# Weights loaded in place, two transposed input tiles and a new dealing-out of the work at the phase boundaries, in a fused attention and MLP kernel

## The chip, the cores and the metric

One core of a Trainium2 chip runs the whole program. The time is the device time of one execution in microseconds, median of the runs shown. TensorE is called PE here, VectorE DVE, ScalarE ACT, GpSimd POOL; SP is the engine that issues the transfers.

## What is computed

x is 16 batches of 128 tokens by 512 numbers, enc the same shape. Two layers follow each other, all in float32:

```
ln  = layernorm(x);   q, k, v = split(ln @ w_qkv + b_qkv)
x   = x + attention(q, k, v, mask_a) @ w_ao + b_ao            # stage A
q   = layernorm(x) @ w_q + b_q;  k, v = split(enc @ w_kv + b_kv)
x   = x + attention(q, k, v, mask_b) @ w_co + b_co            # stage B
x   = x + gelu(layernorm(x) @ w1 + b1) @ w2 + b2              # MLP
a   = layernorm(enc)
x   = x + tanh(gate) * (attention(x @ Wq.T, a @ Wk.T, a @ Wv.T, key mask) @ Wo.T)   # stage D
```

Each attention has 16 heads of 32; in stages A and B the scores are multiplied by the mask and get -10000 * (1 - mask) before the softmax; the gelu is the one with tanh.

## The kernel before, in words

**Products.** Each float32 product is made of three PE passes over split operands: hi by hi, hi by lo, lo by hi. So each weight exists twice on chip, in `weights_hi` and `weights_lo`. The weights are 20 units of 512 x 512, each of four chunks of 128 x 512, which pass in turn through 8 slots. A chunk is loaded by SP (`load_chunk`, L403) into one of four stage buffers, `weights_raw`; ACT rounds it into `weights_hi` (`split`, L980), and POOL (L1735) or, at the start and at the end of the MLP, DVE (L1310) subtracts and writes `weights_lo`. The stage buffer is then free for another chunk. ACT also waits for the slot to be free (`slot_free`).

**Fills.** Inputs come in fills of 256 tokens. For a layer-norm fill, SP loads two tiles, DVE takes the statistics (L1319), POOL the inverse deviation, DVE normalises (`normalise`, L1327, two instructions), SP stores the result to memory (L370) and loads it back with the roles of rows and columns exchanged in blocks (`load_transposed`, L393, four transfers) into the one tile `inputs_transposed`. DVE turns the 32 x 32 blocks in that tile (`turn_inputs`, L1334), ACT applies scale and bias (`fill_scale`, L1078), DVE rounds to the high part (`fill_hi`, L1358) and POOL subtracts the low part (`fill_lo`, L1754). Raw fills, of enc in B and of the stream in D, skip the layer norm. The next transposed load waits until the fill before it has left the tile.

**Steps.** A, B and D have 16 steps each, one batch per step; the batch in the step is called g, 0 to 47 over the three stages. In a step PE makes, in this order: probabilities by v for g-2 (L672), scores of g (L621), one unit of a projection for a later fill (L599, L605), a small product that lays out the row sums of g-1 (L655), two of four transposes of the probabilities of g-1 (L639), a second unit, the other transposes, a third unit, and the output projection of g-2 (L696). DVE and ACT bring out what PE made: `mask_scores` (L1384), POOL `add_mask_bias` (L1764), DVE `row_max` (L1397), ACT `exps` (L1043, 16 instructions), DVE `inverse_sums` (L1405), and from the projections ACT `half_out` for queries and keys (L1009, L1013) and DVE `v_out` for values (L1435). The order on each engine is written out by hand and semaphores alone join them, so an instruction that waits holds up all that stands behind it on its engine.

**Joints.** The MLP works on 64 pairs p: w1 (L752) makes a piece of the hidden layer, ACT `hidden_out` (L1121, L1127) and `tanh` (L1108), DVE the rest of the gelu (L1459 to L1476), w2 (L776) its share of the output. Its first pairs run within the last steps of B (`last_steps_of_b`), and the first projections of D run within its last pairs. There the regular order breaks: in B the steps b = 12 to 15 have fewer projection units left, twelve weight chunks of units 11 to 14 are loaded and split late (table `LATE`), and at the end of the MLP the splits of units 16 to 18 are dealt out by `LAST_SPLITS`.

The lines that set the order of a fill and a chunk in the step of SP are these:

```
if st.weight:
    load_chunk(st.weight)
...
if st.ahead:
    load_transposed(st.ahead)
```

## Time and profile before

| | us |
|---|---|
| Median of three runs | 1167.53 (1167.33 to 1167.87) |
| The profiled execution | 1163.93 |
| Its span | 1162.6 |
| PE busy | 1118.7 (96%) |
| DVE busy | 830.8 (71%) |
| ACT busy | 721.5 (62%) |
| POOL busy | 460.9 (40%) |

The granted clock of PE was 0.997 of full over the profiled execution. Stage A fills about 33 to 281 us of the span, B reaches to about 547, overlapping with the MLP that ends about 903, and D starts within the MLP's last pairs and ends with the span. The table says how much of the span each engine worked, not what it waited for; the waits are read from the rows below.

### The profile page before, as it was taken

What the parts mean: (1) busy time and instruction counts of PE and PEld (TensorE: products, weight loads), DVE (VectorE), ACT (ScalarE), POOL (GpSimd) and SP (SyncE); (2) the same over time, 40 slices, a digit from 0 to 9 for tenths busy, and PEclk for the clock granted to TensorE, in tenths of its full rate; (3) what the DMA queues carried; (4) which work ended last, traced back from release to release, by engine and by line L of the source; (5) the groups of instructions that cost most, each with busy time, mean ns of one, the idle gap of its engine ahead of it and who ended that gap; (6) DMA issues with size and microseconds to landing.
All of it is one profiled execution on the core that took longest, in us unless ns stands there. A gap on an engine that the chain in (4) does not pass through costs nothing.

```text
span 1162.6 us, 26097 instructions
## 1 busy us (share of the span) xinstructions
PE 1118.7 (96%) x9701; PEld 998.1 (86%) x9701; DVE 830.8 (71%) x1351; ACT 721.5 (62%) x2450; POOL 460.9 (40%) x337
## 2 busy tenths in 40 slices
PE   7899999999999999889999999999999989999998
PEld 6788888988888889777799999999998888888886
DVE  6677777677777887797766566655668487777677
ACT  4577776767787777677444434434445286777766
POOL 3675565556667776567412112111111421222100
PEclk9999999999999999899999999999999999999999
DMA  6334443345544445645230230330425445555422
GB/s 205 113 107 121 127 119 93 111 133 147 144 141 135 140 143 148 159 118 160 90 92 19 73 91 1 91 91 1 127 64 160 102 83 130 126 129 123 97 79 83
DMA packets 226238, 128.36 MB, mean 110 GB/s; under 512 B 169680, under 2 KB 177088, under 8 KB 226112
## 3 DMA queue, kind: packets, MB, share of 16 engines
q1 hardware_dynamic: 226112, 126.69, 39.3%
q8 instruction: 78, 1.28, 0.4%
q14 instruction: 48, 0.39, 0.1%
HBM read 93.75 MB, written 32.89 MB: 109 GB/s over the span
## 4 chain that ended last, share of the span: by engine, by line
PE 62%; DVE 12%; ACT 11%; issue 4%; DMA 3%; POOL 3%; SPq 2%; DVEq 0%; ACTq 0%; POOLq 0%
PE psum L605 13%; PE psum L776 13%; PE psum L752 13%; PE psum L696 7%; ACT prob L1043 6%; PE psum L599 5%; PE psum L639 4%; PE psum L621 3%; DVE ln_tile L1327 2%; ACT inputs_transposed L1078 2%; PE psum L672 2%; DVE prob L1384 2%; POOL prob L1764 1%; SPq L393 1%; DMA weights_raw<-weights_in 1%
## 5 line engine op out<-in xcount | busy, mean ns | idle before, releaser
L1043 ACT ACTIVATE prob<-prob,negmax 128x128 f32<-128x128 f32 x768 | 296.8, 393 | 25.6 <-DVE negmax L1397 25.5
L1754 POOL TENSOR_TENSOR inputs_lo<-inputs_transposed,inputs_hi 128x512 fp32r<-128x512 f32 x92 | 124.6, 1374 | 367.0 <-DVE inputs_hi L1358 295.4
L605 PE MATMUL psum<-inputs_hi,weights_hi 128*128 128x256 f32 x768 | 224.6, 292 | 4.6 <-POOL inputs_lo L1754 1.9
L605 PE MATMUL psum<-inputs_lo,weights_hi 128*128 128x256 f32 x768 | 217.0, 283 | 0.0
L605 PE MATMUL psum<-inputs_hi,weights_lo 128*128 128x256 f32 x768 | 216.9, 282 | 0.0
L1764 POOL TENSOR_TENSOR prob<-prob,mask_bias 128x1024 f32<-128x1024 f32 x64 | 155.4, 2450 | 135.6 <-DVE prob L1384 133.5
L605 PEld LDWEIGHTS psum<-inputs_hi,weights_hi 128*128 128x128 f32 x768 | 146.6, 191 | 9.5 <-issue 2.8
L1043 ACT ACTIVATION_READ_ACCUMULATOR prob<-prob,negmax 128x1 f32 x768 | 148.0, 193 | 0.0
L605 PEld LDWEIGHTS psum<-inputs_lo,weights_hi 128*128 128x128 f32 x768 | 146.9, 191 | 0.2
L605 PEld LDWEIGHTS psum<-inputs_hi,weights_lo 128*128 128x128 f32 x768 | 146.8, 191 | 0.0
L752 PE MATMUL psum<-inputs_hi,weights_hi 128*128 128x256 f32 x512 | 145.0, 283 | 1.0 <-POOL inputs_lo L1754 1.0
L752 PE MATMUL psum<-inputs_lo,weights_hi 128*128 128x256 f32 x512 | 144.9, 283 | 0.0
L752 PE MATMUL psum<-inputs_hi,weights_lo 128*128 128x256 f32 x512 | 144.9, 283 | 0.0
L1397 DVE TENSOR_REDUCE negmax<-prob 128x8 f32<-128x1024 f32 x96 | 113.4, 1199 | 17.2 <-POOL prob L1764 17.1
L1121 ACT ACTIVATE qT<-psum,columns 128x256 f32<-128x256 f32 x128 | 53.4, 469 | 112.7 <-PE psum L752 112.7
L1476 DVE SCALAR_TENSOR_TENSOR kT<-kT,qT 128x512 f32<-128x512 f32 x64 | 53.0, 829 | 92.1 <-ACT kT L1127 91.9
L776 PE MATMUL psum<-weights_hi,context_hi 128*128 128x512 f32 x256 | 101.4, 396 | 5.7 <-DVE context_lo L1471 5.5
L752 PEld LDWEIGHTS psum<-inputs_hi,weights_hi 128*128 128x128 f32 x512 | 98.0, 191 | 3.6 <-issue 1.2
L639 PE MATMUL psum<-identity,prob 128*128 128x128 f32 x752 | 98.2, 273 | 2.8 <-ACT prob L1032 2.4
L776 PE MATMUL psum<-weights_lo,context_hi 128*128 128x512 f32 x256 | 100.4, 392 | 0.0
L752 PEld LDWEIGHTS psum<-inputs_lo,weights_hi 128*128 128x128 f32 x512 | 98.0, 191 | 2.3
L776 PE MATMUL psum<-weights_hi,context_lo 128*128 128x512 f32 x256 | 99.7, 389 | 0.0
(112 smaller groups left out, 2526.6 us busy)
## 6 DMA issues: line engine op xcount, KB each, us to landing
weights_raw<-weights_in SPq DMA_DIRECT2D x72, 256.0 KB, 4.0
normalised<-ln_tile SPq DMA_DIRECT2D x30, 512.0 KB, 2.8
inputs_transposed<-normalised SPq DMA_DIRECT2D x120, 128.0 KB, 3.4
stream<-residual SPq DMA_DIRECT2D x48, 256.0 KB, 2.9
residual<-stream SPq DMA_DIRECT2D x48, 256.0 KB, 3.8
context<-row_sums_spread SPq DMA_DIRECT2D x188, 64.0 KB, 2.0
ln_tile<-stream SPq DMA_DIRECT2D x32, 256.0 KB, 3.8
ln_tile<-x_in SPq DMA_DIRECT2D x16, 256.0 KB, 3.4
```

The lines of the kernel that those rows point to most:

```text
L599: mm = pe.matmul(ps[:, bank, :], a[:, buf, c, tok], w[:, slot, c, :], start=c == 0 and i == 0, stop=c == KC - 1 and i == 2)
L605: mm = pe.matmul(ps[:, bank, GT * part:GT * part + GT], w[:, slot, c, o], a[:, buf, c, :], start=c == 0 and i == 0, stop=c == KC - 1 and i ...
L639: mm = pe.transpose(ps[:, bank, T * j:T * j + T], prob[:, g % 2, s:s + T], ident[:, :])
L696: mm = pe.matmul(ps[:, U_BANK + 1, :], a[:, 0, cs], w[:, slot, c, :], start=c == 0 and i == 0, stop=c == KC - 1 and i == 2)
L752: mm = pe.matmul(ps[:, bank, GT * e:GT * e + GT], w[:, slot, c, o], a[:, gp, c, :], start=n == 0, stop=n == 3 * KC - 1)
L776: mm = pe.matmul(ps[:, acc, :], a[:, gb, tok], w[:, slot, 2 * (j % 2) + e, :], start=j == 0 and n == 0, stop=j == NPAIR - 1 and n == 5)
L1043: ins = act.activation(P[:, T * s:T * s + T], P[:, T * s:T * s + T], ACT.Exp, bias=negmax[:, par, s:s + 1], accum_out=total[:, par, s:s + 1])
L1121: ins = act.activation(hx(p)[:, GT * e:GT * e + GT], ps[:, bank, GT * e:GT * e + GT], ACT.Identity, bias=cols[:, col:col + 1])
L1397: dve.tensor_reduce(negmax[:, par, 8 * h:8 * h + 8], heads(prob[:, par, 1024 * h:1024 * h + 1024]), AX.X, ALU.max, negate=True).then_inc(s ...
L1476: dve.scalar_tensor_tensor(hw(p), hw(p), 1.0 / GELU_A, hx(p), ALU.add, ALU.mult).then_inc(s_in, 1)
L1754: pool.tensor_tensor(xlo[:, fill.buf, :, tokens(t)], y, xhi[:, fill.buf, :, tokens(t)].bitcast(f32), ALU.subtract).then_inc(s_rlo if fill. ...
L1764: pool.tensor_tensor(half, half, mb.unsqueeze(1).to_broadcast([128, 8, T]), ALU.add).then_inc(s_biased, 1)
```

## The change

**Weights.** The stage buffers are gone. A chunk is loaded straight into the place where its low part will stand: `weights_whole` is a plain float32 view of the memory of `weights_lo`. ACT reads it there for `weights_hi`, and the subtraction overwrites it in place. So SP, not ACT, now waits for the slot to be free, and the chunk of the following step is loaded a step ahead. `LATE` is gone: B loads two chunks in steps 5 and 11, units 13 and 12 at the end of step 13, unit 14 after step 15; the units 16 to 19 have new places and splits, more of them on DVE.

**Fills.** `inputs_transposed` has two tiles, used in turn; a transposed load waits for the fill two before it.

**Order.** In B, steps 12 and 13 take three units instead of two, and 14 and 15 none: two pairs of w1 stand in their place. The DVE's `normalise` moves behind the row maxima, `turn_inputs` behind the first of them. ACT brings out the second unit before `fill_scale`. In D the first two steps of ACT are written out anew. PE makes the same products.

```diff
@@ attention_steps, steps of B
+        elif phase == B and b < 14:
+            units = [(phase, 7, n) for n in ((0, 1, 2), (4, 5, 3))[odd]]
...
-        elif phase == B:
-            units = [None, (phase, 7, (2, 3)[odd]), None]
...
+        elif phase == B and b < 14:
+            chunks = [b + (b > 5) + (b > 11)] + ([b + 1 + (b > 5)] if b in (5, 11) else [])
...
-LAST_SPLITS = {2: (16, 0), 3: (16, 2), 4: (17, 0), 5: (17, 2), 6: (18, 0), 7: (18, 2)}
+LAST_SPLITS = {3: (16, 0), 4: (16, 2), 5: (17, 0), 6: (17, 2), 7: (18, 0)}
@@ build, tiles
         whi = sb("weights_hi", [128, SLOTS, KC, H], f32r)
+        with nc.sbuf_tensor("weights_whole", [128, SLOTS, KC, H], f32) as raw:
+            pass
         wlo = sb("weights_lo", [128, SLOTS, KC, H], f32r)
-        raw = sb("weights_raw", [128, STG, H])
...
-        xt = sb("inputs_transposed", [128, KC, GT])
+        xt = sb("inputs_transposed", [128, 2, KC, GT])
...
-            return g in (0, 28, 32, 44)
+            return g in (0, 32, 44)
@@ SP
             def load_transposed(fill):
-                was = PREVIOUS[fill]
+                was = FILLS[FILLS.index(fill) - 2]
...
+            def slot_free(unit):
+                if unit in (8, 9, 10, 11):
+                    sp.wait_ge(s_half, half_count(A, 7, 5))
...
+                if unit in (16, 18):
+                    sp.wait_ge(s_h, 60 if unit == 18 else 58)
+                if unit in (17, 19):
+                    sp.wait_ge(s_w2, 58 if unit == 17 else 60)
             def load_chunk(chunk):
...
-                sp.dma_start(raw[:, buf, :], weights[chunk[0], chunk[1], :, :]).then_inc(s_raw[buf], 16)
+                sp.dma_start(raw[:, slot_of(unit), c, :], weights[unit, c, :, :]).then_inc(s_raw[k], 16)
...
-                if st.weight:
-                    load_chunk(st.weight)
+                for chunk in following.weights if following else []:
+                    load_chunk(chunk)
...
-                if st.phase == B and st.b >= 13:
-                    for chunk in LATE[st.b + 1][:3]:
-                        load_chunk(chunk)
+                if st.phase == B and st.b == 13:
+                    for unit in (13, 12):
+                        for c in range(KC):
+                            load_chunk((unit, c))
...
-                    unit = {(0, 6): 15, (6, 7): 16, (7, 2): 17, (7, 5): 18}.get((g, jp))
+                    unit = {(0, 6): 15, (7, 2): 16, (7, 3): 17, (7, 5): 18}.get((g, jp))
...
             load_transposed(raw_fill(D, 0, 0))
+            load_transposed(ln_fill(3, 1, 1))
...
-            load_transposed(ln_fill(3, 1, 1))
             load_transposed(STEPS[D][0].fill)
@@ PE, last_steps_of_b
-                    if b == 14:
-                        row_sums_out(28)
                     w1_bank_free(2 * b - 28)
                     w1(2 * b - 28)
                     row_sums(g - 1)
                     transpose_prob(g - 1, 0)
                     transpose_prob(g - 1, 1)
                     row_sums_out(g - 1)
-                    project(*unit, U_BANK + 1)
+                    w1(2 * b - 27)
                     transpose_prob(g - 1, 2)
                     transpose_prob(g - 1, 3)
-                    w1_bank_free(2 * b - 27)
-                    w1(2 * b - 27)
-                    half_out(*unit)
+                    pe.wait_ge(s_hx, 2 * b - 26)
                     project_out(g - 2)
                 times_v(30)
-                w2(0)
+                w1_bank_free(4)
+                w1(4)
                 row_sums(31)
                 transpose_prob(31, 0)
                 transpose_prob(31, 1)
+                w2(0)
@@ ACT, step
+                if st.fill and st.fill not in TURNED:
+                    fill_hi(st.fill)
+                if not st.prev or (st.ends and not late):
+                    half_out(*st.units[1])
+                if st.fill in TURNED:
+                    fill_out(st.fill)
+                if st.prev:
+                    prob_out(g - 1, 2)
+                if not st.ends:
+                    half_out(*st.units[2])
                 exps(g, 0)
...
@@ DVE, step
-                if st.ahead and st.ahead.ln is not None:
+                if ahead_ln and later_ln:
                     normalise(st.ahead)
-                if st.fill in TURNED:
-                    turn_inputs(st.fill)
-                row_max(g, 0)
+                if st.ends or not st.prev:
+                    row_max(g, 0)
+                    if st.fill in TURNED:
+                        turn_inputs(st.fill)
...
                 if st.prev:
                     prob_out(g - 1, 3)
+                if ahead_ln and not later_ln:
+                    normalise(st.ahead)
@@ DVE, end of the MLP
-                if g == NG - 1 and jp in LAST_SPLITS:
+                if g == NG - 1 and jp in (3, 4):
                     unit, c = LAST_SPLITS[jp]
                     split((unit, c))
                     split((unit, c + 1))
             turn_inputs(raw_fill(D, 0, 0))
             gelu_hi(NG * NPAIR - 1)
             gelu_lo(NG * NPAIR - 1)
+            for unit in (17, 18):
+                for c in range(KC):
+                    split((unit, c))
             mlp_out(NG - 1)
```

DVE in an odd step of stage A, where the fill ahead is normalised (`ln_tile` is its tile, `negmax` the row maxima, `v` the values of a projection). Before:

```order
L1384 SCALAR_TENSOR_TENSOR prob<-psum,mask 128x512 x4
L1410 COPY prob<-psum 128x512
L1327 TENSOR_SCALAR ln_tile<-ln_tile,ln_mean_var,ln_rstd 128x512 x2
L1397 TENSOR_REDUCE negmax<-prob 128x8
L1435 TENSOR_TENSOR v<-psum,bias_rows 128x512
L1397 TENSOR_REDUCE negmax<-prob 128x8
L1410 COPY prob<-psum 128x512
L1435 TENSOR_TENSOR v<-psum,bias_rows 128x512
L1447 TENSOR_TENSOR residual<-psum,residual 128x512
```

After:

```order
L1380 SCALAR_TENSOR_TENSOR prob<-psum,mask 128x512 x4
L1406 COPY prob<-psum 128x512
L1393 TENSOR_REDUCE negmax<-prob 128x8
L1431 TENSOR_TENSOR v<-psum,bias_rows 128x512
L1393 TENSOR_REDUCE negmax<-prob 128x8
L1406 COPY prob<-psum 128x512
L1322 TENSOR_SCALAR ln_tile<-ln_tile,ln_mean_var,ln_rstd 128x512 x2
L1431 TENSOR_TENSOR v<-psum,bias_rows 128x512
L1443 TENSOR_TENSOR residual<-psum,residual 128x512
```

The two `normalise` instructions moved behind both row maxima and the first of the two `v_out`.

DVE in step 12 of stage B, before:

```order
L1384 SCALAR_TENSOR_TENSOR prob<-psum,mask 128x512 x4
L1410 COPY prob<-psum 128x512
L1327 TENSOR_SCALAR ln_tile<-ln_tile,ln_mean_var,ln_rstd 128x512 x2
L1334 STREAM_TRANSPOSE inputs_transposed<-inputs_transposed 128x1024
L1397 TENSOR_REDUCE negmax<-prob 128x8 x2
L1410 COPY prob<-psum 128x512
L1358 CAST inputs_hi<-inputs_transposed 128x4x128 x2
```

The same place after:

```order
L1380 SCALAR_TENSOR_TENSOR prob<-psum,mask 128x512 x4
L1406 COPY prob<-psum 128x512
L1393 TENSOR_REDUCE negmax<-prob 128x8
L1329 STREAM_TRANSPOSE inputs_transposed<-inputs_transposed 128x1024
L1393 TENSOR_REDUCE negmax<-prob 128x8
L1406 COPY prob<-psum 128x512
L1322 TENSOR_SCALAR ln_tile<-ln_tile,ln_mean_var,ln_rstd 128x512 x2
L1353 CAST inputs_hi<-inputs_transposed 128x4x128 x2
```

The turn no longer stands behind `normalise`; the fill that is turned here was normalised a step earlier, and the one that is normalised here is the next.

ACT in step 14 of stage B, the first with MLP work in it (`qT` and `kT` hold the hidden layer there), before:

```order
L1064 ACTIVATE context_hi<-context 128x256 x2
L1052 ACTIVATE row_sums_transposed<-psum 16x128
L1032 ACTIVATE prob<-psum 128x512
L980 ACTIVATE weights_hi<-weights_raw 128x512 x3
L1121 ACTIVATE qT<-psum,columns 128x256 x2
L1127 ACTIVATE kT<-qT 128x512
L1043 ACTIVATE prob,total<-prob,negmax 128x128 x4
L1032 ACTIVATE prob<-psum 128x512
L1043 ACTIVATE prob,total<-prob,negmax 128x128 x4
L1121 ACTIVATE qT<-psum,columns 128x256 x2
L1127 ACTIVATE kT<-qT 128x512
L1043 ACTIVATE prob,total<-prob,negmax 128x128 x8
```

The same place after:

```order
L1049 ACTIVATE context_hi<-context 128x256 x2
L1037 ACTIVATE row_sums_transposed<-psum 16x128
L1106 ACTIVATE qT<-psum,columns 128x256 x2
L1112 ACTIVATE kT<-qT 128x512
L1017 ACTIVATE prob<-psum 128x512
L980 ACTIVATE weights_hi<-weights_whole 128x512 x2
L1106 ACTIVATE qT<-psum,columns 128x256 x2
L1112 ACTIVATE kT<-qT 128x512
L1017 ACTIVATE prob<-psum 128x512
L1028 ACTIVATE prob,total<-prob,negmax 128x128 x16
```

Three chunk splits became two, and both `hidden_out` stand ahead of the sixteen exponentials.

## Rows read from the trace of the kernel before

**Rows 1.** Windows: stretch, length; busy PE, PEld, DVE, ACT, POOL; clock; DMA share; GB/s

```profile
40.00:62.00 22.00, 17.62 (x191) 15.24 (x191) 15.47 (x25) 16.21 (x68) 14.90 (x10) 1.00 0.41 116
62.00:470.00 408.00, 404.48 (x3998) 359.91 (x3998) 315.09 (x518) 301.49 (x1170) 260.00 (x172) 1.00 0.46 131
470.00:530.00 60.00, 51.06 (x478) 44.34 (x478) 48.67 (x71) 41.90 (x150) 37.03 (x23) 0.94 0.50 142
530.00:585.00 55.00, 49.88 (x343) 42.59 (x342) 43.57 (x54) 30.49 (x81) 29.22 (x20) 1.00 0.33 105
585.00:885.00 300.00, 300.00 (x1928) 274.00 (x1927) 186.23 (x298) 127.06 (x246) 47.14 (x42) 1.00 0.24 68
885.00:955.00 70.00, 62.56 (x513) 55.96 (x512) 47.58 (x75) 37.75 (x115) 23.66 (x20) 1.00 0.49 118
```

**Rows 2.** Timeline, 471 to 481 us (start, length, instruction, idle before)

```profile
471.77 4.89 POOL L1764 TENSOR_TENSOR prob<-prob,mask_bias 128x1024 f32<-128x1024 f32 x2 [2.46 <-DVE prob L1384]
...
473.40 3.54 DVE L1327 TENSOR_SCALAR ln_tile<-ln_tile,ln_mean_var,ln_rstd 128x512 f32<-128x512 f32 x2
476.87 1.23 DVE L1334 STREAM_TRANSPOSE inputs_transposed<-inputs_transposed 128x1024 f32<-128x1024 f32 x1
...
478.13 2.07 ACT L1078 ACTIVATE inputs_transposed<-inputs_transposed,columns 128x256 f32<-128x256 f32 x4 [3.35 <-DVE inputs_transposed L1334]
...
480.98 0.79 PE L696 MATMUL psum<-weights_hi,context_hi 128*128 128x512 f32 x1 [5.55 <-ACT kT L1013]
```

**Rows 3.** Windows, line L696 alone, the stretch right behind that wait

```profile
481.00:486.50 5.50, 5.46 (x12) 3.77 (x12) 0.50 0.19 30
```

**Rows 4.** Waits of PE, 530 to 585 us (total, times, longest)

```profile
PE psum L776 <- DVE context_lo L1471: 4.0, 4, 1.2
PE psum L696 <- DVE context_lo L1421: 1.0, 1, 1.0
```

**Rows 5.** Part 5 of the page, the exponentials on ACT

```profile
L1043 ACT ACTIVATE prob<-prob,negmax 128x128 f32<-128x128 f32 x768 | 296.8, 393 | 25.6 <-DVE negmax L1397 25.5
```

**Rows 6.** Waits of PE, 85 to 190 us

```profile
PE psum L696 <- DVE v L1435: 3.0, 4, 1.3
```

**Rows 7.** Waits of PE, 885 to 955 us

```profile
PE psum L621 <- ACT qT L1009: 2.6, 2, 2.0
PE psum L776 <- DVE context_lo L1471: 1.5, 2, 1.0
```

**Rows 8.** Timeline, SP and DVE at the end of the MLP

```profile
872.08 18.39 SPq L403 DMA_DIRECT2D weights_raw<-weights_in  x8
...
916.12 1.25 DVE L1334 STREAM_TRANSPOSE inputs_transposed<-inputs_transposed 128x1024 f32<-128x1024 f32 x1 [10.12 <-DMA inputs_transposed<-normalised]
```

**Rows 9.** Timeline of DVE, two instructions with and without POOL beside them

```profile
862.45 0.99 DVE L1327 TENSOR_SCALAR ln_tile<-ln_tile,ln_mean_var,ln_rstd 128x512 f32<-128x512 f32 x2
...
886.63 3.49 DVE L1310 TENSOR_TENSOR weights_lo<-weights_raw,weights_hi 128x512 fp32r<-128x512 f32 x2
```

**Rows 10.** Timeline, two steady steps of stage B, 396 to 425 us

```profile
396.38 3.07 DVE L1327 TENSOR_SCALAR ln_tile<-ln_tile,ln_mean_var,ln_rstd 128x512 f32<-128x512 f32 x2
...
403.12 2.78 SPq L393 DMA_DIRECT2D inputs_transposed<-normalised  x4
...
411.75 1.23 DVE L1334 STREAM_TRANSPOSE inputs_transposed<-inputs_transposed 128x1024 f32<-128x1024 f32 x1
...
413.69 2.07 ACT L1078 ACTIVATE inputs_transposed<-inputs_transposed,columns 128x256 f32<-128x256 f32 x4
...
414.92 1.22 DVE L1397 TENSOR_REDUCE negmax<-prob 128x8 f32<-128x1024 f32 x1 [0.84 <-POOL prob L1764]
...
422.44 0.26 DVE L1405 RECIPROCAL rtotal<-total 128x16 f32<-128x16 f32 x1 [1.67 <-ACT prob L1043]
...
424.20 0.27 PE L655 MATMUL psum<-identity,rtotal 128*16 128x128 f32 x1
```

**Rows 11.** Part 6 of the page: transfers, KB each, us from issue to landing

```profile
inputs_transposed<-normalised SPq DMA_DIRECT2D x120, 128.0 KB, 3.4
```

More of the change, by code:

```diff
@@ L15 @@
 SLOTS = 8
-STG = 4
 EPS = 1e-5
@@ L42 @@
 Fill = namedtuple("Fill", "ln phase q buf n")
-Step = namedtuple("Step", "phase b prev ends units fill weight ahead later")
+Step = namedtuple("Step", "phase b prev ends units fill weights ahead later")
 def ln_fill(ln, q, buf):
@@ L1501, in step @@
                     context(g - 2, 1)
+                if st.ends and not late and phase == D:
+                    make_mask_bias(g)
+                    mask_scores(g, 0)
+                if st.ends and not late:
                     inverse_sums(g - 1)
@@ L1718, in dve_program @@
             gelu_lo(NG * NPAIR - 1)
+            for unit in (17, 18):
+                for c in range(KC):
+                    split((unit, c))
             mlp_out(NG - 1)
```

292 lines of the change are left out of this document (136 added, 156 removed).

## The prediction

> **What bounds the kernel now.** First the windows. PE is busy 300.00 us of the 300 in the middle of the MLP and 404.48 of 408 from 62 to 470 us [rows 1]. Since the change leaves PE the same products, nothing is to be won where PE never stops; the time can only come out of its gaps. They lie together: 4.38 us between 40 and 62, 3.52 from 62 to 470, 8.94 in 470 to 530, 5.12 in 530 to 585 and 7.44 in 885 to 955 [rows 1], 29.4 in all. The other engines are at most 71% busy, so a gap is an order in which something stands too late. The waits and the timeline then say which order. What is in those gaps is the most that the change can win, beside a clock that falls behind one of them.
>
> **The change part by part, end of B and entry of the MLP.** The largest gap ends at 480.98 after 5.55 us: the first product of an output projection waits for the kT copy of ACT [rows 2]. The timeline shows why. DVE's two normalise instructions start at 473.40 and take 3.54 us beside POOL's mask additions (471.77, 4.89), the turn of another fill stands behind them at 476.87, and ACT, which has idled 3.35 us for that turn, does fill_scale from 478.13 for 2.07 us and only then the copy [rows 2]. The change undoes this twice: the turn no longer stands behind a normalise in that step, and the copy stands ahead of fill_scale. Without fill_scale ahead of it alone the copy could come at least 5 us earlier, so I take the gap as gone. Behind the gap the 12 products of that line took 5.46 us at a granted clock of 0.50, that is 1.2 of the two levels 1.2 and 2.4 GHz [rows 3]. Halving that gives 2.73 back; the bounds are 0 (another gap drops the clock as well) and 2.73, and I take it whole, since no other gap in these stretches is as long.
>
> The rest of the idle time of 470 to 530 is 3.4 us in small waits, and 530 to 585 has four waits of w2 for the gelu, 4.0 us, and one of 1.0 [rows 4]. Steps 14 and 15 now have two w1 pairs in place of pair and unit, both hidden copies ahead of the exponentials, and two splits instead of three. So the gelu is earlier and w2 should wait little. In exchange the exponentials, which are 296.8 us over 48 steps, so 6.2 a step [rows 5], start later: behind two hidden copies, a projection's worth of ACT work that was spread through them. ACT's chain of a step is then about as long as PE's work in it, and I leave 1.9 us for row sums and products with v of the last two steps that wait for it, and 3 us for small waits: about 5 stay of 14.1. The sum for this part is -(14.1 - 5) - 2.7 = -11.8; call it **-12**. The end least favourable, only the 5.55 gap and no clock, is -5.5.
>
> **Stage A.** Between 85 and 190 us PE waits four times, 3.0 us, for the `v` copy of DVE [rows 6]; in each of these steps the copy stands behind a normalise of up to 3.58 us beside the additions. The change puts the first of the two copies ahead of the normalise and I take these 3.0 as gone, with 0.3 of smaller ones: **-3.3**. The bounds are 0, if the second copy, still behind the normalise, is as late, and -3.5. In the first steps, where 4.38 us are lost [rows 1], g = 1 gets the turn and the copies ahead; what is left is the wait for the first row sums, which is a chain of exponentials that the change leaves. I take **-1.5**, between 0 and -4.4.
>
> **End of the MLP and entry of D.** SP now waits for the fill two before, and the last layer-norm fill of D is loaded right behind the first raw one instead of behind residuals and chunks. Before, DVE idled 10.12 us for it until 916.12 [rows 8], and ACT's qT copy behind it held PE for 2.6 us in two waits [rows 7]. That wait goes, and with it most of 5.9 us of gaps without w2 in that stretch; I leave 1, so about -5. Against it stand the weights. Before, eight chunk loads took 18.39 us to issue, from 872.08, since each waited for a stage buffer [rows 8]; now they are issued when the slot is free, unit 16 one pair later than before, and ACT's split in pair 3 of the last group stands behind their landing. What is queued behind that split is the gelu chain that w2 waits for, 1.5 us in two waits already [rows 7]. I add 1.4 us. The eight splits that DVE gets in one run before `mlp_out(7)` cost between 4 (two of another form in 0.99) and 14 us (two in 3.49 beside POOL) [rows 9]; they lie beside PE's first projections of D and, as long as those last, at nothing. Net **-3.6**, between -6 and +2.
>
> **Steady steps of B.** Here the change costs. The normalise starts at 396.38 now and ends 399.45, the transposed loads are issued from 403.12 to 405.90, and their turn stands at 411.75 [rows 10]; a load lands 3.4 us after its issue [rows 11]. Moved behind both row maxima and a copy the normalise starts about 401.0, and takes 0.99 to 3.58 us [rows 2, 9], so it ends 2.6 to 5.1 us later than now. Against this stand some 3.1 us of slack at the turn (411.75 less the landing of the fourth load, about 405.2 + 3.4), and 1.9 more since the turn itself moves behind a row maximum: the second waits 0.84 for POOL until 414.92, the first can start one addition (2.45) earlier, at about 412.5, and the turn ends at 414.9 instead of 413.0 [rows 2, 10]. So the loads should just be in time. fill_scale then starts at 414.9 and not at 413.69, 1.2 us later; the row sums are ready at 422.7 and PE takes them at 424.20, which leaves 1.5 [rows 10]. So the shift is hidden with 0.3 us to spare. That cover is thin, and I book **+0.5** for all such steps, between 0 and +9 (13 layer-norm fills by 0.7). Stage A has the same order, but there fill_scale already stands behind copies, so I book nothing.
>
> The normalise takes 0.99 us alone at 862.45 and 3.54 beside the additions [rows 2, 9]. The Trainium skill, SBUF — State Buffer, "Who interferes with whom", says that DVE and GpSimd share a port pair that one holds for a whole instruction while the other fully blocks. By that rule the moved normalise, now beside POOL's `fill_lo` and residual bias, would wait for whole instructions of POOL, which speaks for the late end of the range above and gives the rival of lateness below; the rows agree in size, but none here shows the pair at the new place.
>
> **In place loading.** It removes no work of ACT, DVE or POOL. The chunks of A and B are loaded a step ahead; where ACT waited for landings between copies it now doesn't, and this lies beside PE's work: nothing, both ways.
>
> **Sum**: -12 - 3.3 - 1.5 - 3.6 + 0.5 = -19.9. The profiled execution took 1163.93 us, 3.6 under the median 1167.53; its own time would become 1144.0. Against the median that is **1148 us**, rounded up as all the terms lean on whole gaps.
>
> **Rivals.** (a) *Lateness in the LN fills*: the moved normalise delays store, loads and turn beyond the slack in the steps with a layer-norm fill, at 0.7 us in 13 of them: +9, so about 1157. For it: 0.3 us to spare and DVE beside POOL. Against it: the load slack grows with the turn. (b) *The boundaries pay half*: ACT's exponentials bound the last steps of B and unit 16 comes late, so 6 to 7 of the 15.6 us of the two boundaries stay: 1154 or 1155. For it: ACT's chain there is as long as PE's. (c) *Slower*: SP's queue. Normalise late means that store, four loads, row sums' store and spread behind them on SP are all late, so that DVE's context waits as well as its turn, in all layer-norm fills of A, B and D, some 20. It decides from 1.05 us per fill beyond the slack, where it eats the 20 us; at 1.5 us it is +30 - 20: 1177. Against it: the spread has other time, and the largest shift found is 5.1 against 5.0. (d) *It doesn't do what it says*: the gaps only move, since PE waits for what was second latest each time: about 1167. Against it: the largest gap has two causes and both are removed.
>
> **How the numbers follow.** Forecast case 0.62 (1142 to 1152), (a) 0.17, (b) 0.14, (c) 0.04, (d) 0.03. The low end is 1142, where A's first steps and the entry of the MLP give all they have; the high end 1158 takes in (a) and (b). About 0.2% or 2.3 us is what a measurement of this kernel can tell from no change. Faster than 1165.2 by that: 0.93; within: 0.03; slower: 0.04.
>
> **What would show it.** The windows 470 to 530 and 530 to 585 with PE at some 95% and a clock near 1.00; no wait of L696 for kT above 1 us; in stage A no waits for `v`; DVE's idle time at D's second turn gone. Wrong: in each second step of B a gap at the row sums, or waits of the turn for its transfer, say (a); a wait of ACT's split for weights in the last group with w2 idle says (b); spread transfers waited for by DVE in every pair say (c).

## The result: 1137.85 us, and the profile after

The changed kernel took 1137.85 us (median of 4, 1137.55 to 1138.20) against 1167.43 of the kernel before in the same comparison (4 runs, 1166.68 to 1167.87): a ratio of 0.9747, 95% interval 0.973 to 0.9764. The forecast was 1148, range 1142 to 1158. The direction was right, the gain half as large again as forecast, and the range missed.

The profiled execution took 1137.63 us with a span of 1136.3. PE is busy 1112.6 us of it (98%), DVE 826.8, ACT 719.5, POOL 459.7. The windows of the changed kernel around the places that [rows 1] show (columns as there):

```profile
40.00:62.00 22.00, 19.90 (x210) 17.32 (x209) 17.39 (x30) 19.30 (x81) 15.06 (x11) 1.00 0.46 118
467.00:520.00 53.00, 52.02 (x526) 45.94 (x525) 47.31 (x72) 45.41 (x174) 36.65 (x24) 1.00 0.54 156
520.00:570.00 50.00, 46.16 (x293) 39.63 (x292) 37.96 (x49) 24.45 (x53) 28.82 (x20) 1.00 0.26 87
865.00:925.00 60.00, 57.48 (x477) 51.59 (x476) 46.22 (x69) 38.46 (x114) 24.34 (x20) 1.00 0.46 108
```

PE idles 2.10 us in the first steps (4.38 before), 0.98 and 3.84 around the end of B (8.94 and 5.12), and 2.52 at the entry of D (7.44); the clock is 1.00 in all of them, where [rows 1] had 0.94. The waits of PE from 520 to 570 us, where [rows 4] had 4.0 and 1.0:

```profile
PE psum L782 <- DVE context_lo L1467: 1.7, 2, 1.6
PE psum L678 <- ACT prob L1017: 0.8, 1, 0.8
PE psum L758 <- POOL weights_lo L1746: 0.8, 1, 0.8
PE psum L661 <- DVE rtotal L1401: 0.5, 1, 0.5
```

To see where time went, the starts of the same PE product in the two traces serve better than windows. These are the rows of the changed kernel (timeline of PE; start and length first), the first scores of batches 5, 16, 28, 35, 44 and 47 and the first w2 product of pairs 8 and 57:

```profile
105.29 0.39 PE L627 MATMUL psum<-kT,qT 32*128 32x128 f32 x4
...
274.44 0.39 PE L627 MATMUL psum<-kT,qT 32*128 32x128 f32 x4
...
459.36 0.39 PE L627 MATMUL psum<-kT,qT 32*128 32x128 f32 x4
...
573.02 0.40 PE L782 MATMUL psum<-weights_hi,context_hi 128*128 128x512 f32 x1
...
848.39 0.40 PE L782 MATMUL psum<-weights_hi,context_hi 128*128 128x512 f32 x1
...
938.17 0.39 PE L627 MATMUL psum<-kT,qT 32*128 32x128 f32 x4
...
1076.86 0.39 PE L627 MATMUL psum<-kT,qT 32*128 32x128 f32 x4
...
1113.35 0.39 PE L627 MATMUL psum<-kT,qT 32*128 32x128 f32 x4
```

| up to | before at | after at | stretch won | forecast |
|---|---|---|---|---|
| scores of batch 5 | 108.79 | 105.29 | 3.50 | 1.5 |
| batch 16 | 280.85 | 274.44 | 2.91 | 3.3 |
| batch 28 | 466.46 | 459.36 | 0.69 | -0.5 |
| w2 of pair 8 | 593.04 | 573.02 | 12.92 | 12 |
| w2 of pair 57 | 868.42 | 848.39 | 0.01 | 0 |
| batch 35 | 963.16 | 938.17 | 4.96 | 3.6 |
| batch 44 | 1101.85 | 1076.86 | 0.00 | 0 |
| batch 47 | 1139.64 | 1113.35 | 1.30 | 0 |
| end of the span | 1162.6 | 1136.3 | 0.0 | 0 |

Batch here is g, counted over the three stages. The stretches add up to 26.3 us, where the sum had 19.9. The other 3.3 of the 29.6 lie between the profiled execution of before (1163.93) and its timed runs.

The place of the largest gap, [rows 2], reads like this now (timeline, DVE, then ACT, then PE, in step 12 of B):

```profile
468.75 1.23 DVE L1329 STREAM_TRANSPOSE inputs_transposed<-inputs_transposed 128x1024 f32<-128x1024 f32 x1
...
471.71 1.00 DVE L1322 TENSOR_SCALAR ln_tile<-ln_tile,ln_mean_var,ln_rstd 128x512 f32<-128x512 f32 x2
...
467.47 0.84 ACT L998 ACTIVATE kT<-psum,columns 128x256 f32<-128x256 f32 x2 [1.76 <-PE psum L611]
470.02 2.08 ACT L1063 ACTIVATE inputs_transposed<-inputs_transposed,columns 128x256 f32<-128x256 f32 x4 [1.72 <-DVE inputs_transposed L1329]
...
470.89 0.39 PE L702 MATMUL psum<-weights_hi,context_hi 128*128 128x512 f32 x1
```

ACT's copy runs at 467.47, ahead of fill_scale, the turn stands behind one row maximum only, and the normalise, now behind both and with POOL idle beside it, takes 1.00 us instead of 3.54. The third unit gives PE work from 468.06 on, and it goes into its output projection at 470.89 without a wait.

### The profile page after: what moved, and what is told of

The parts are those of the page before. It is cut to its first block, busy times and chain, and to the rows that moved or that the text cites. A ratio compares the mean times of both kernels' runs of the same rounds, so it can differ in the third digit from the quotient of the medians.

```text
span 1136.3 us, 26121 instructions
## 1 busy us (share of the span) xinstructions
PE 1112.6 (98%) x9701; PEld 996.5 (88%) x9701; DVE 826.8 (73%) x1351; ACT 719.5 (63%) x2450; POOL 459.7 (40%) x337
## 4 chain that ended last, share of the span: by engine, by line
PE 78%; DVE 7%; ACT 7%; DMA 3%; issue 2%; POOL 2%; SPq 1%; DVEq 0%; ACTq 0%
PE psum L611 20%; PE psum L758 13%; PE psum L782 13%; PE psum L702 9%; PE psum L605 9%; PE psum L645 6%; PE psum L627 4%; ACT prob L1028 4%; PE psum L678 3%; POOL prob L1775 1%; ACT inputs_transposed L1063 1%; DMA weights_whole<-weights_in 1%; DMA normalised<-ln_tile 1%; DVE context_lo L1467 1%; DVE prob L1380 1%
## 5 line engine op out<-in xcount | busy, mean ns | idle before, releaser
L1775 POOL TENSOR_TENSOR prob<-prob,mask_bias 128x1024 f32<-128x1024 f32 x64 | 153.0, 2413 | 119.5 <-DVE prob L1380 117.5
```

The source lines that it names most:

```text
L1775: pool.tensor_tensor(half, half, mb.unsqueeze(1).to_broadcast([128, 8, T]), ALU.add).then_inc(s_biased, 1)
```

## The experiments

Ratios are to the kernel before, run on the same chip, with their 95% intervals; for edits of the changed kernel the distance to its own 1137.85 (1138.03 when it ran again, below) says more. The kernel before had medians of 1164.4 to 1165.6 in these later comparisons. Labels that begin with b_ are the kernel before with an edit, those with a_ the changed kernel with one.

**The largest gap by itself, in the kernel before.** First both swaps in g = 28:

```diff
@@ DVE, step
+                if g == 28:
+                    turn_inputs(st.fill)
                 if st.ahead and st.ahead.ln is not None:
                     normalise(st.ahead)
-                if st.fill in TURNED:
+                if st.fill in TURNED and g != 28:
                     turn_inputs(st.fill)
@@ ACT, step
+                if g == 28:
+                    half_out(*st.units[1])
                 if st.fill and not regular:
                     fill_out(st.fill)
-                if not st.prev or not (st.units[2] or late):
+                if not st.prev or (not (st.units[2] or late) and g != 28):
                     half_out(*st.units[1])
```

> The kernel before with two changes in step 12 of stage B alone (g = 28): DVE turns ahead of normalise, ACT copies the second unit ahead of fill_scale. Theory 1: the whole 5.55 us gap goes and the clock with it, and the 3.5 us by which the timed runs of before lie over its profiled execution are also a clock lost behind this gap; then the median falls by 5.5 + 2.7 + 3.5 = 11.7 us, to about 1156, and the span of the profiled execution by 8.3. Theory 2: those 3.5 us belong to timed runs as such (or to something else in the program); then the median falls by 8.3, to about 1159. Theory 3: the gap only moves to the row sums or to the gelu; then under 3 us are won.

Measured: 1161.17 us (1159.19 to 1165.82), ratio 0.997 (0.9956 to 0.9985). Theory 3 came nearest: 3.3 us, and the gap moved. Its timeline (DVE, ACT, ACT, PE; the profiled execution is the slowest of its eleven) shows what it moved to:

```profile
475.85 3.67 DVE L1329 TENSOR_SCALAR ln_tile<-ln_tile,ln_mean_var,ln_rstd 128x512 f32<-128x512 f32 x2
...
480.69 0.40 ACT L1043 ACTIVATE prob<-prob,negmax 128x128 f32<-128x128 f32 x1 [2.00 <-DVE negmax L1399]
...
482.24 0.57 ACT L1032 ACTIVATE prob<-psum 128x512 f32<-128x512 f32 x1
...
482.87 1.51 PE L672 MATMUL psum<-prob,v 128*32 128x128 f32 x24 [3.05 <-ACT prob L1032]
```

The exponentials wait 2.00 us for row maxima that stand behind a normalise of 3.67; the copy of the third block of probabilities (L1032), which this step put behind the first quarter of the exponentials, comes at 482.24; PE waits 3.05 us for it. So the gap had a third cause behind the two that I had found. Then the ACT part of that diff alone (b_act28) and the DVE part alone (b_dve28):

> The kernel before with ACT's copy ahead of fill_scale in g = 28 and nothing else. If the copy's place alone made the gap, this is worth all that both are worth (8.3 to 11.7 us). If the late turn still holds fill_scale, the exponentials and the row sums of g = 28, 2 to 4 us come back as a wait one step later and 5 to 8 are won.

> The kernel before with DVE's turn ahead of normalise in g = 28 and nothing else. fill_scale then ends at about 476.7 instead of 480.2 and the copy at 477.5, so a gap of some 2 us stays; 3.5 us are won if the clock still falls behind it, 6 to 9.5 if it doesn't. The other theory (normalise beside POOL just blocks elsewhere, and the next fill is late): nothing won.

Measured: ACT's swap 1163.51 us, ratio 0.9994 (0.9982 to 1.0006), nothing that can be told; DVE's 1161.51, ratio 0.9967 (0.9956 to 0.9979), 2.9 us. With ACT's swap alone the same product by v waits 4.05 us. Theories with 5 us and more fall for both.

**The changed kernel with one part undone.**

First DVE's order:

```diff
@@ DVE, step
-                if ahead_ln and later_ln:
+                if ahead_ln:
                     normalise(st.ahead)
                 if st.ends or not st.prev:
-                    row_max(g, 0)
                     if st.fill in TURNED:
                         turn_inputs(st.fill)
+                    row_max(g, 0)
...
-                if ahead_ln and not later_ln:
-                    normalise(st.ahead)
```

> The changed kernel with DVE's normalise back ahead of the row maxima and the turn back ahead of the first row maximum. By my account this gives back the 2.9 us of stage A (waits for v) and, in g = 28 and 29, what the turn behind normalise costs: with ACT's copy ahead of fill_scale only 0 to 3 us there. So 1141 to 1144. Rival: the DVE order is what removes the big gap, then 1146 or more. B's steady steps: no difference by either.

Measured: 1143.96 us, ratio 0.982 (0.9801 to 0.9839): 6.1 us back. By the starts of the scores 2.8 of them lie in stage A, where the wait for `v` returns (first row below, 85 to 190 us, against [rows 6]), 0.8 at the end of B, and 2.5 in D's second step, where the second row's wait is new:

```profile
PE psum L702 <- DVE v L1431: 2.2, 4, 0.6
...
PE psum L605 <- ACT v L1007: 2.4, 1, 2.4
```

Then ACT's, with the rule of before for `regular` steps:

```diff
@@ ACT, step
-                if st.fill and st.fill not in TURNED:
-                    fill_hi(st.fill)
-                if not st.prev or (st.ends and not late):
-                    half_out(*st.units[1])
-                if st.fill in TURNED:
-                    fill_out(st.fill)
...
+                if st.fill and not regular:
+                    fill_out(st.fill)
+                if not st.prev or not (st.units[2] or late):
+                    half_out(*st.units[1])
+                if late:
+                    prob_out(g - 1, 2)
+                if regular:
+                    half_out(*st.units[1])
+                if st.fill and regular:
+                    fill_out(st.fill)
```

> The changed kernel with the order of ACT's step as before (second unit behind fill_scale where the third is missing, second and third unit among the exponentials in the first steps). All steps 12 and 13 of B have three units now, so the old rule takes its regular branch there and the big gap does not come back: 1138 to 1139. What comes back is the first steps: 0.5 to 1.5 us. Rival: ACT's order carries the boundary, then 1143 or more.

Measured: 1139.59 us, ratio 0.9779 (0.9763 to 0.9795): 1.7 us back, 1.2 of them in D's step 12, where the copy stands behind fill_scale again (not in the first steps, as expected), and none at the end of B.

One tile instead of two:

```diff
-TILE_OF = {_fill: _n % 2 for _n, _fill in enumerate(FILLS[2:])}
+TILE_OF = {_fill: 0 for _fill in FILLS[2:]}
...
-                was = FILLS[FILLS.index(fill) - 2]
+                was = FILLS[FILLS.index(fill) - 1]
```

> The changed kernel with one transposed tile again: each load waits for the fill just before it. In B's steady steps the loads landed 0.17 us before the turn could use them with two tiles, so if the second tile is what lets them be in time, each layer-norm fill of B loses, and D's second fill is late again as before: 3 to 5 us lost at D and 0 to 5 in B, so 1141 to 1148. Rival: the store of the normalised tile, not the free tile, sets the load (it waits 3.5 us for the store's landing), so only the entry of D loses, or nothing: 1138 to 1141.

Measured: 1140.66 us, ratio 0.9788 (0.9772 to 0.9804): 2.8 us back, all but a few tenths at D's entry. In B's steps one is 0.3 us longer and the others are as they were: from 285 to 460 us SP waits 12.2 us for the stores of normalised tiles to land and 0.7 for the tile to be free, so the store sets the load there, not the tile.

The place of one load:

```diff
             load_transposed(raw_fill(D, 0, 0))
-            load_transposed(ln_fill(3, 1, 1))
...
             load_tiles(ln_fill(3, 2, 1))
+            load_transposed(ln_fill(3, 1, 1))
             load_transposed(STEPS[D][0].fill)
```

> The changed kernel with the transposed load of the last layer-norm fill of D back behind the residual and chunk loads. If its early place is what won the 5 us at D's entry, 3 to 5 us come back: 1141 to 1143. If the second tile alone did it, nothing.

Measured: 1148.24 us, ratio 0.9853 (0.9838 to 0.9869): 10.4 us back, more than any theory said. The wait of PE between 855 and 930 us, and the clock in it:

```profile
PE psum L611 <- ACT v L1007: 9.4, 1, 9.4
...
904.00:907.00 3.00, 1.83 (x8) 1.83 (x9) 2.30 (x7) 1.60 (x4) 1.82 (x2) 0.50 0.04 6
```

PE waits 9.42 us for a `v`, since in the changed order ACT's fill_scale of that fill stands ahead of that copy and waits for the load, and PE goes on at a clock of 1.2 GHz. The early load is not a bonus there; the new ACT order needs it.

**The units of B's last steps.**

ACT's and DVE's order in steps 14 and 15 is the old one too, as far as these units need it: the hidden copies stand among the exponentials again.

```diff
         elif phase == B and b < 14:
-            units = [(phase, 7, n) for n in ((0, 1, 2), (4, 5, 3))[odd]]
+            units = [(phase, 7, (0, 4)[odd]), (phase, 7, (1, 5)[odd]), None]
+        elif phase == B:
+            units = [None, (phase, 7, (2, 3)[odd]), None]
@@ PE, last_steps_of_b
-                    w1(2 * b - 27)
+                    project(B, 7, b - 12, U_BANK + 1)
                     transpose_prob(g - 1, 2)
                     transpose_prob(g - 1, 3)
+                    w1_bank_free(2 * b - 27)
+                    w1(2 * b - 27)
```

> The changed kernel with the projection units of B's last four steps dealt as before: two in steps 12 and 13, one in 14 and 15, with the first w1 pairs, the hidden copies and the copy of that unit in their old places; weights in place, two tiles, DVE and ACT orders of the regular steps as in the change. Theory 1, from the first four of these runs: a step of B with two units gives PE 12.5 us of work against some 13 of ACT with its exponentials, so PE waits in step 12 for the copies of the probabilities, whatever stands in front of them; the third unit is what fills the gap. Then 6 to 12 us come back: 1144 to 1150, with a wait before the products with v at g = 28 and more at w2. Theory 2: the orders of the regular steps and the weights in place carry it: under 3 us come back.

Measured: 1142.78 us, ratio 0.981 (0.9796 to 0.9823): 4.9 us back, 4.4 of them by the trace between batch 28 and the first w2. Waits of PE from 465 to 570 us:

```profile
PE psum L684 <- ACT prob L1025: 3.2, 3, 1.6
PE psum L788 <- DVE context_lo L1475: 1.7, 2, 1.5
PE psum L617 <- POOL inputs_lo L1774: 1.0, 1, 1.0
```

The products with v wait 3.2 us for copied probabilities. Between the two theories: the units, with the order of steps 14 and 15 that goes with them, carry 4.4 of the 12.9 us, not 6 to 12.

**The load a step ahead.** In the changed kernel without it (a_own_step), and in the kernel before with it (b_ahead), both in SP's step:

```diff
@@ a_own_step
-                for chunk in following.weights if following else []:
+                for chunk in st.weights if g else []:
                     load_chunk(chunk)
@@ b_ahead
-                if st.weight:
-                    load_chunk(st.weight)
+                following = (STEPS[A] + STEPS[B])[g + 1] if g < 31 else None
+                if g == 0:
+                    load_chunk(st.weight)
+                if following and following.weight:
+                    load_chunk(following.weight)
```

> The changed kernel with each chunk of A and B loaded in its own step instead of the one before. If the landing of a chunk, which ACT waited for between copies, cost time before, 1 to 5 us come back and the runs spread again over several microseconds as those of before do (1160.8 to 1168.3). If it was hidden, as the prediction has it: 1138, spread under 1.5.

> The kernel before with its four stage buffers, each chunk of A and B loaded in the step before its own; nothing else. Theory 1: the ACT of before hides its chunk waits in the old order (its waits for chunks are 27.6 us in all and PE hardly stops there), so the load ahead alone wins 0 to 2 us, and is only what allows the new order. Theory 2: the load ahead is itself the gain: 5 us or more, with the spread of the runs gone.

Measured: a_own_step 1165.52 us (1162.71 to 1168.12), ratio 1.0004 (0.9991 to 1.0016). The changed kernel loses 27.5 us by it, far more than either theory said. b_ahead 1163.97 us, ratio 0.9985 (0.9976 to 0.9994): 1 us. The waits of ACT for chunks, in the changed kernel and in a_own_step:

```profile
ACT weights_hi L980 <- DMA weights_whole<-weights_in: 11.1, 6, 5.4
```

```profile
ACT weights_hi L980 <- DMA weights_whole<-weights_in: 78.9, 20, 6.7
```

78.9 us against 11.1 (27.6 in the kernel before). In the new order `split` stands ahead of the copies of the projection, so a chunk that lands late holds up what PE waits for: from batch 4 to 28 most steps are 0.5 to 2.3 us longer, one 3.9, 27.0 in sum. This is a loss that the kernel before doesn't have (its batch 28 starts at 466.46 us, that of a_own_step at 487.10); the gain behind batch 28 stays, and that the two cancel to a ratio of 1.00 is chance. Theory 1 holds for b_ahead: early loading wins next to nothing in the old order. It is the condition of the new one.

Two more go on from b_ahead: b_ahead28 adds the two swaps of the first diff, and b_orders the change's regular order of ACT and DVE for all steps:

```diff
@@ ACT, step
-                if not st.prev or not (st.units[2] or late):
+                if not st.prev or (st.ends and not late):
                     half_out(*st.units[1])
...
@@ DVE, step
+                if ahead_ln and later_ln:
+                    normalise(st.ahead)
+                row_max(g, 0)
                 if st.fill in TURNED:
                     turn_inputs(st.fill)
-                row_max(g, 0)
...
+                if ahead_ln and not later_ln:
+                    normalise(st.ahead)
```

> The same load ahead, and the two swaps in g = 28 (turn ahead of normalise, copy ahead of fill_scale). The swaps alone won 3.3 us. If the chunk's landing was the next thing late there, together they win clearly more than the two apart: 6 to 9. If the missing third unit is, 3 to 5.

> The kernel before with the load ahead and the regular step orders of ACT and DVE from the change; stage buffers, one tile, the old units in B's last steps and the old MLP end stay. Stage A should win its 2.9 us, g = 28 the big gap less what two units leave (about 5 of the 12.9 us of that boundary by the run with the old units), so 8 to 11 us: 1154 to 1157. If it wins under 5, the places of loads and splits around the boundary (table LATE) carry the rest.

Measured: b_ahead28 1159.83 us, ratio 0.9958 (0.9945 to 0.9972): 5.1 us, at the end of the 3 to 5 that the missing third unit was to leave. b_orders 1162.98 us, ratio 0.9983 (0.9974 to 0.9991): 1.9 us only. Its trace has the gains that were expected: 2.7 us ahead up to batch 16, and 6.2 won from batch 28 to w2 of pair 8, of which 2.7 are the clock that doesn't fall there. But it loses 2.9 again in the first steps of B (a wait of 2.23 for a copy of probabilities on DVE) and 6.0 from batch 32 to 44. D's steps lack the change's earlier mask and its second tile there; which of them it is was not tested. So the order of steps pays only with more of the change around it.

**D's entry in the kernel before.**

```diff
             load_transposed(raw_fill(D, 0, 0))
+            load_transposed(ln_fill(3, 1, 1))
...
             load_tiles(ln_fill(3, 2, 1))
-            load_transposed(ln_fill(3, 1, 1))
```

> The kernel before with one thing moved: the transposed load of the last layer-norm fill of D right behind the first raw one, still with one tile. The 2 us wait before the first scores of D goes and with it the clock that falls behind it in some executions: 3 to 6 us won. Rival: with one tile the load waits for the raw fill to leave it, and SP with it, so that residual and chunk loads behind it are late: nothing won, or slower.

Measured: 1161.40 us (1159.58 to 1162.52), ratio 0.9967 (0.9956 to 0.9979): 3.9 us. The largest wait of the first scores fell from 2.0 [rows 7] to 0.9.

**The gaps that are left.**

a_split16 puts ACT's four splits of unit 16 in pair 4 behind fill_scale, and DVE's in pair 5. a_plus2 puts both in pair 4, ACT's ahead of fill_scale, and moves two transposes:

```diff
@@ a_plus2: ACT, loop over the pairs (DVE the same, in pair 4)
+                if g == NG - 1 and jp == 4:
+                    for c in range(KC):
+                        split((16, c))
                 if jp == (5 if g == 0 else 4):
                     fill_scale(FILLS_OF_MLP[g] or mlp_fill(1))
...
-                if g == NG - 1 and jp in LAST_SPLITS:
+                if g == NG - 1 and jp > 4:
@@ a_plus2: PE, last_steps_of_b
-                project_out(30)
                 transpose_prob(31, 2)
                 transpose_prob(31, 3)
+                project_out(30)
```

a_plus has besides, on ACT and POOL, unit 14 split before 13, and unit 15 in pair 5 ahead of fill_scale and of fill_lo.

> The changed kernel with the four splits of unit 16 at one place, a pair later on ACT (in pair 4 of the last group) and in pair 5 on DVE. ACT no longer waits 5.39 us for the landing of the first chunk in pair 3. If that wait is what costs 0.56 of w2 there, it goes; four splits in a row take ACT 2.3 us and may cost as much a pair later: 1136.5 to 1139.

Measured: 1138.54 us, ratio 0.9771 (0.9757 to 0.9786), no better: one wait of w2 of 2.24 us for two of 0.56 and 1.02, with a granted clock of 0.67 in the 4 us around its end (872 to 876 us).

> The changed kernel with five moves at gaps that its trace still shows: unit 14 split before 13 (w1 waits 0.78 us for POOL), unit 15 split a pair earlier and ahead of fill_scale and fill_lo (w2 waits 1.54), the last two transposes of batch 31 ahead of the output projection of 30 (0.83), and the four splits of unit 16 together in pair 4 ahead of fill_scale, where ACT idles for the turn (0.56 and 1.02). If each gap goes and none comes new: 4.4 us, about 1133.5. If POOL's splits beside DVE's gelu just slow it a pair earlier: 2 us or less.

Measured: 1137.46 us, ratio 0.9763 (0.975 to 0.9775). By the trace the transposes won 0.9 and the splits of unit 16 2.0. From batch 28 to w2 of pair 8 the kernel is all the same 2.6 us longer than a_plus2, the next run, which has these two moves and not the splits of 13 to 15. Part of that is DVE beside POOL a pair earlier, as the second theory said: the waits of w2 there are 4.0 us in sum and not 1.8. The rest is a granted clock that falls to 0.73 around the end of the longest of them (556 to 560 us), less a wait of w1 of 0.8 that is gone.

> The changed kernel with only the two moves that won in the run before: the last two transposes of batch 31 ahead of the output projection of 30, and the four splits of unit 16 together in pair 4 ahead of fill_scale on ACT. Units 13 to 15 are split where the change has them. In the traces those two were worth 0.9 and 2.1 us, so 1134.6 to 1135.3, a clock of 1.00 and a spread under 1.5 us.

> The changed kernel as it is, again, on the chip of the run beside it: 1137 to 1138.5, with the kernel before at 1161 to 1168 on the same chip. If the chips of the first runs were unlike, the ratio of 0.9747 moves by the 2 to 3 us by which the first four runs of before lie over the later ones.

Measured: a_plus2 1135.16 us (1134.82 to 1135.78), ratio 0.9742 (0.9729 to 0.9756); a_same 1138.03 (1137.62 to 1138.49), ratio 0.9766 (0.9753 to 0.9779), before 1165.56 (1162.98 to 1166.53). a_plus2 is 2.9 us faster than the change and the fastest version here. The change itself is worth 27.5 us in this comparison; the first runs of before lay at the upper end of what it does.

## Why the prediction was wrong

**What bounds the kernel.** Right: PE's work is the same, and the gain came at the places listed. PE's idle time fell by 20.2 us (from 43.9 to 23.7), and its busy time by 6.1, of which 2.7 are the clock behind the largest gap. What failed is the sum, in two steps. First, its terms were too small: -19.9, where the same stretches gave -26.3. The first steps gave 2.0 us more than booked, D's entry 1.4, the steady steps of B 1.2, the end of B 0.9, and the end of D 1.3 for which there was no term; stage A gave 0.4 less. Second, "Against the median that is 1148 us" added the 3.6 between one profiled execution and the median as if it were a constant; measured, these 3.3 us came back on top. The terms weigh more: without the constant the forecast is 1144.0, still 6.2 too high.

**One execution and the median.** In later runs before took 1160.8 to 1168.3 us, with medians 2 to 3 us under the first one, and the change 1137.6 to 1138.5. So the distance is no constant; it lies within a spread that the changed kernel doesn't have. In the profiled execution of before only one gap was followed by the lower clock [rows 3]. In b_dve28, which differs from it in one place of DVE's order, the clock isn't down there but behind a w2 wait and at D's entry (windows, columns as in [rows 1]):

```profile
555.00:558.00 3.00, 3.00 (x9) 2.28 (x9) 2.27 (x4) 0.63 (x1) 0.00 (x0) 0.53 0.84 288
919.00:925.00 6.00, 5.20 (x46) 5.01 (x39) 5.80 (x11) 1.14 (x4) 5.92 (x7) 0.72 0.57 90
```

Of the seven profiles of the kernel before and its edits that load D's last fill as before, five show the lower clock there; before and b_both28 don't. So each execution loses the clock behind another few of its gaps, while the changed kernel's two profiled runs had 1.00 throughout. In the 85 later runs of before the time goes with the mean clock: a median of 1166.4 us at 0.991 to 0.993 (13 runs), 1165.2 at 0.994 (37) and 1163.9 above (35). It isn't all of it. The runs at 0.994 alone lie up to 5 us apart (1163.1 to 1168.3), and a_own_step spreads from 1162.7 to 1168.1 at clocks of 0.996 to 1.000, its slowest run at 0.999. What the rest is stays open.

**End of B: -12 forecast, -12.92 measured.** The size was right by luck in part, since the reason was not. "I take the gap as gone": it is, but not by the two causes named. Both removed in the kernel before won 3.3 us, since the copy of the probabilities stood behind the first exponentials, those behind a row maximum, and that behind the normalise. The argument that failed is the one under rival (d), "the largest gap has two causes and both are removed": there was at least a third behind them. The change also moves this copy ahead of the exponentials and the normalise behind the maxima. By the traces the regular orders with the early load (b_orders) win 6.2 us in this stretch, 2.7 of them the clock, and the units with the order of steps 14 and 15 are worth 4.4. The remaining 2.3 no run separates; the new places of loads and splits in B's last steps lie there. Undone alone in the changed kernel, DVE's order costs only 0.8 us at the end of B and ACT's none, so with the third unit in the step the third cause hardly shows.

**Stage A: -3.3, measured -2.91.** Right in place, mechanism and size; undone alone, 2.8 us come back.

**First steps: -1.5, measured -3.50**, of which 0.75 lies ahead of the first scores (33.34 us in before, 32.59 in the changed kernel) and can't be put down to the change: in the profiles of the changed kernel and its variants they start between 32.59 and 33.70. The other 2.75 are won in the steps. The two waits of 1.07 and 2.08 us there became one of 1.00, ahead of the row sums. The term was undersized, inside its bound of 4.4.

**D's entry: -3.6, measured -4.96.** The parts: w2 pairs 57 to 60 lose 1.8 us (forecast 1.4), and from there 6.8 are won (forecast 5). What I didn't see is that ACT's new order makes the early load necessary: without it 10.4 us are lost. The eight splits on DVE took 8.27 us, between my 4 and 14, and PE has no wait for them.

**Steady steps of B: +0.5, measured -0.69.** No cost came, but the slack was not the one that I had worked out. The changed kernel at the place of [rows 10], where the same products start 7.13 us earlier (normalise and turn on DVE, POOL's `fill_lo`, ACT's fill_scale, the row sums, and the product that takes them):

```profile
393.50 2.45 DVE L1322 TENSOR_SCALAR ln_tile<-ln_tile,ln_mean_var,ln_rstd 128x512 f32<-128x512 f32 x2
...
404.95 1.25 DVE L1329 STREAM_TRANSPOSE inputs_transposed<-inputs_transposed 128x1024 f32<-128x1024 f32 x1 [0.17 <-DMA inputs_transposed<-normalised]
...
392.93 2.74 POOL L1765 TENSOR_TENSOR inputs_lo<-inputs_transposed,inputs_hi 128x512 fp32r<-128x512 f32 x2
...
406.56 2.07 ACT L1063 ACTIVATE inputs_transposed<-inputs_transposed,columns 128x256 f32<-128x256 f32 x4
...
415.31 0.26 DVE L1401 RECIPROCAL rtotal<-total 128x16 f32<-128x16 f32 x1 [1.03 <-ACT prob L1028]
...
417.07 0.27 PE L661 MATMUL psum<-identity,rtotal 128*16 128x128 f32 x1
```

With 7.13 added, the normalise starts at 400.6 and ends 3.6 us later than before, as I had it, and the slack of the loads is used up: the turn waits 0.17 us for them. But the turn starts at 412.1 and not at 413.7, since DVE waits less for the exponentials and begins the step's masks 2.0 us earlier, and fill_scale starts at 413.69 as before, right behind a copy of ACT. So the row sums keep the whole 1.5 us ahead of PE, and the "0.3 us to spare" was never drawn on: the forecast held by a shift that I had not seen. The Trainium skill's rule on the port pair (SBUF — State Buffer, "Who interferes with whom"), weighed in the prediction, says that one engine holds the pair for a whole instruction while the other is blocked. The trace agrees in direction: the normalise beside `fill_lo` took 2.45 us and not 0.99. What I left out are 0.7 us that the first steps of B gain.

**End of D: left out, measured -1.30.** I had a wait of L696 for kT there, 0.9 us, and no term for it. Undoing ACT's order gives 1.2 back.

**In place loading: "nothing, both ways".** The worst of the reasons, though the number hid it. I asked what the early load saves where it is, and not what the moved instructions behind it would wait for. It wins 1 us in the old order, and leaving it out costs 27 in the new.

**The rivals.** (a) did not come; (b) came in small, 1.8 us at unit 16; (c) did not: in the changed kernel PE has no wait over 0.2 us between 85 and 465 us; (d) came true in the kernel before with the two swaps, not in the change.

The range failed because its low end, 1142, let only the first steps and the entry of the MLP give all they had. What came at D's entry, at the end of D and in the steady steps lay outside it, and so did the distance of the median.

## What to carry to other kernels

A gap has as many causes as there are instructions standing late in front of it; follow the chain past the first release, and ask what each queue runs next, before taking the gap as gone. A load that costs nothing in one order can be the condition of another: when copies move behind a wait, cost that wait anew. And where runs of a kernel spread by several microseconds, a prediction for one that waits less should say what becomes of the spread, and not carry the distance of one execution over as a constant.

## What the runs showed of the hardware

DVE's gelu instructions slow down while POOL splits weights, and POOL with them. Timeline of the changed kernel at the entry of the MLP (DVE, POOL, DVE, DVE):

```profile
539.00 1.67 DVE L1467 SCALAR_TENSOR_TENSOR context_lo<-kT,context_hi 128x512 fp32r<-128x512 f32 x1
...
532.55 12.65 POOL L1746 TENSOR_TENSOR weights_lo<-weights_whole,weights_hi 128x512 fp32r<-128x512 f32 x8 [3.57 <-ACT weights_hi L980]
...
475.72 1.29 POOL L1746 TENSOR_TENSOR weights_lo<-weights_whole,weights_hi 128x512 fp32r<-128x512 f32 x1
...
560.94 0.68 DVE L1467 SCALAR_TENSOR_TENSOR context_lo<-kT,context_hi 128x512 fp32r<-128x512 f32 x1
```

The eight splits take POOL 1.58 us each and not 1.29 as one alone does (475.72), and the same DVE instruction takes 1.67 us beside them and 0.68 at 560.94. This bears on the splits of unit 15 a pair earlier, in what looked like idle time of POOL: in a_plus the instruction took 1.75 us at 546.81, in a_plus2, without them, 0.68 at 545.33. So POOL's idle time beside DVE was not free here. The other surprise was the run to run spread: 7.5 us for before, about 1 us for the change, with the same transfers and the same work.
